# Inverting the softmax denominators of an attention kernel in a folded 128x16 tile

## What is computed

```python
xn = _layernorm(x, axis=-1)                       # x: (2, 2048, 512)
q, k, v = split(xn @ W_qkv); per head of 32
attn = q @ k.T / sqrt(32) + alibi_bias + causal_mask
y = softmax(attn) @ v                             # heads side by side, then @ W_o
x = x + y @ W_o + gate * (expert_out[argmax] + b)
```

## Time and profile before

| | us |
|---|---|
| median of three runs | 1879.65 |
| lowest, highest | 1877.83, 1888.87 |
| the profiled execution's own time | 1884.69 |
| its span, first to last instruction | 1883.1 |
| PE busy | 1731.0 (92%) |
| DVE busy | 1092.8 (58%) |
| ACT busy | 799.8 (42%) |
| POOL busy | 678.4 (36%) |
| mean granted clock of PE | 0.955 |

### The profile page before, as it was taken

How to read it: one execution, slowest core, us unless ns; L and a number is a source line. 1 busy time by engine, 2 the same in 40 slices (tenths; PEclk the granted TensorE clock), 3 DMA queues, 4 the chain that set the end, 5 groups by cost and what they waited for, 6 DMA issues and landing times. The chain is left out here.

```text
span 1883.1 us, 31814 instructions
## 1 busy us (share of the span) xinstructions
PE 1731.0 (92%) x10482; PEld 1057.3 (56%) x10483; DVE 1092.8 (58%) x1969; ACT 799.8 (42%) x1575; POOL 678.4 (36%) x668
## 2 busy tenths in 40 slices
PE   5999999568699999999999899999999999699798
PEld 4777778334254555554554555555555543588676
DVE  5333333556576766766766667766766730544365
ACT  3222222024344555555565456556555556421110
POOL 4401000036433454354355246246245346011350
PEclk8999999669899999999999899999999999899899
DMA  6766764875901801900900900720730500355594
GB/s 224 247 224 228 261 213 159 147 202 198 182 6 35 155 8 26 164 8 15 176 8 9 182 8 7 144 46 7 142 49 7 186 12 7 117 181 164 181 395 188
DMA packets 103621, 231.34 MB, mean 123 GB/s; under 512 B 10828, under 2 KB 28236, under 8 KB 97836
## 3 DMA queue, kind: packets, MB, share of 16 engines
q1 hardware_dynamic: 87736, 178.83, 36.8%
q0 software_dynamic: 15744, 50.67, 7.5%
HBM read 131.09 MB, written 97.85 MB: 122 GB/s over the span
## 5 line engine op out<-in xcount | busy, mean ns | idle before, releaser
L957 DVE TENSOR_REDUCE part_max<-max_ps 128x1 f32<-128x512 f32 (+3 forms) x1280 | 700.7, 602 | 375.5 <-PE max_ps L1068 272.6
L1038 ACT ACTIVATE probs_sb<-score_ps 128x512 f32<-128x512 f32 (+3 forms) x1280 | 620.5, 542 | 541.4 <-PE score_ps L1106 244.3
L941 POOL TENSOR_TENSOR pair_sum<-probs_sb 128x512 f32<-128x512 f32 x384 | 480.0, 1282 | 587.3 <-ACT probs_sb L1038 463.2
L1068 PE MATMUL max_ps<-k_aug,q_aug 104*128 104x512 f32 (+3 forms) x1280 | 535.5, 429 | 56.8 <-DMA q_aug<-q_rows_d 36.9
L1103 PE MATMUL score_ps<-q_aug,k_aug 106*128 106x512 f32 (+3 forms) x1280 | 523.2, 415 | 28.9 <-ACT probs_sb L1038 12.6
L1103 PEld LDWEIGHTS score_ps<-q_aug,k_aug 106*128 106x128 f32 x1280 | 251.6, 197 | 177.0 <-issue 114.9
L1068 PEld LDWEIGHTS max_ps<-k_aug,q_aug 104*128 104x128 f32 x1280 | 259.1, 203 | 131.9 <-DVE part_max L957 70.6
L1147 PE MATMUL acc_ps<-probs_sb,v_sb 128*32 128x512 f32 (+3 forms) x2560 | 293.5, 537 | 0.0
L989 DVE RECIPROCAL acc_sb<-acc_sb 128x128 f32<-128x128 f32 x128 | 119.8, 941 | 76.6 <-ACT acc_sb L1022 76.6
L1147 PEld LDWEIGHTS acc_ps<-probs_sb,v_sb 128*32 128x32 f32 x2560 | 73.5, 111 | 113.8 <-issue 98.5
L614 DVE SCALAR_TENSOR_TENSOR st_lo<-group_ps,st_hi 128x512 fp32r<-128x512 f32 x64 | 44.3, 692 | 139.6 <-ACT st_hi L661 135.0
(11 more groups left out here) (171 smaller groups left out, 1689.5 us busy)
## 6 DMA issues: line engine op xcount, KB each, us to landing
k_aug<-k_hi_d SPq DMA_DIRECT2D x14, 1024.0 KB
q_aug<-q_hi_d SPq DMA_DIRECT2D x14, 1024.0 KB
slot_x_d<-zero_f POOLq DMA_DIRECT2D x20, 512.0 KB, 5.9
rows<-slot_x_d SPq DMA_DIRECT2D x40, 256.0 KB, 2.6
slot_y_d<-y_rows POOLq DMA_DIRECT2D x39, 256.0 KB, 2.5
xn_d<-xn SPq DMA_DIRECT2D x8, 1024.0 KB, 10.3
q_hi_d<-st_hi SPq DMA_DIRECT2D x32, 256.0 KB, 7.2
q_lo_d<-st_lo SPq DMA_DIRECT2D x32, 256.0 KB, 7.1
```

The source lines that it names most:

```text
L941: nc.gpsimd.tensor_tensor(pair_sum[:, p % 2, hh], probs[:, s0, hh], probs[:, s1, hh], ALU.add).then_inc(pair_added, 1)
L957: nc.vector.tensor_reduce(part_max[:, hh * QT + i, kc:kc + 1], max_ps[:, bank, 0:w], AX.X, ALU.max).then_inc(max_taken, 1)
L1038: nc.scalar.activation(probs[:, r % P_SLOTS, hh, off:CH], score_ps[:, (r * HG + hh) % S_BANKS, off:CH], ACT.Exp).then_inc(exp_done, 1)
L1068: last = nc.tensor.matmul(max_ps[:, bank, 0:w], q_aug[0:ROW_MAX, half, hh, i * P:(i + 1) * P], k_aug[0:ROW_MAX, half, hh, kc * CH:kc * CH ...
```

## The change

The four quarter reciprocals go. ACT, after its exponentials of round 3 past a chunk's last, issues a DMA that takes the four different rows of the denominators (every 32nd partition, 512 numbers) and lays them out as 128 partitions of 16 numbers (`fold_out`, into `den_fold`). DVE inverts that tile in one instruction in round 4 past the last. In round 5 ACT issues a DMA that writes it to DRAM (`unfold`, into `inv_d`), and in round 6 one that reads each of the four rows 32 times, back over `den_sb` (`spread_rows`). POOL's product stands where it stood and waits for that last DMA. All four steps wait on semaphores of the step before. On all other engines the order stays.

```diff
@@ -147,12 +147,17 @@
 
 
 LEAVE_AT = {(LAST_ROUND[c] + 2) % NR: ((LAST_ROUND[c] + 2) // NR, c) for c in range(QC)}
-QUARTERS = 4
-INVERT_AT = {(LAST_ROUND[c] + 3 + k) % NR: ((LAST_ROUND[c] + 3 + k) // NR, c, k)
-             for c in range(QC) for k in range(QUARTERS)}
-
-Y_BEFORE_PAIR = {min([p for p in range(NPAIR) if PAIR_LAST[p] > (LAST_ROUND[c] + 3 + QUARTERS) % NR] or [NPAIR]):
-                 ((LAST_ROUND[c] + 3 + QUARTERS) // NR, c) for c in range(QC)}
+
+
+def rounds_past(n):
+
+    return {(LAST_ROUND[c] + n) % NR: ((LAST_ROUND[c] + n) // NR, c) for c in range(QC)}
+
+
+FOLD_AT, INVERT_AT, UNFOLD_AT, SPREAD_AT = rounds_past(3), rounds_past(4), rounds_past(5), rounds_past(6)
+
+Y_BEFORE_PAIR = {min([p for p in range(NPAIR) if PAIR_LAST[p] > (LAST_ROUND[c] + 7) % NR] or [NPAIR]):
+                 ((LAST_ROUND[c] + 7) // NR, c) for c in range(QC)}
 
 
 class Memory:
@@ -188,6 +193,7 @@
     m.y_d = nc.dram_tensor("y_d", [G, P, S], F32).ap()
     m.slot_x_d = nc.dram_tensor("slot_x_d", [SLOTS, D], F32).ap()
     m.slot_y_d = nc.dram_tensor("slot_y_d", [SLOT_TILES * P, D], F32).ap()
+    m.inv_d = nc.dram_tensor("inv_d", [2, HG, CH], F32).ap()
     m.k_rows_d = nc.dram_tensor("k_rows_d", [AUG_ROWS, H, S], F32).ap()
     m.q_rows_d = nc.dram_tensor("q_rows_d", [AUG_ROWS, HG, S], F32).ap()
 
@@ -755,6 +761,7 @@
         max_lo = sb("max_lo", [HG * TPC, 2, P], F32R)
         acc_sb = sb("acc_sb", [P, 2, 2, CH], F32)
         y_sb, den_sb = acc_sb[:, :, 0], acc_sb[:, :, 1]
+        den_fold = sb("den_fold", [P, 2, HG * CH // P], F32)
         score_ps = pb("score_ps", [P, S_BANKS, CH], F32)
         max_ps = pb("max_ps", [P, M_BANKS, CH], F32)
         acc_ps = pb("acc_ps", [P, 2, CH], F32)
@@ -773,6 +780,7 @@
             sem("scored"), sem("probs_ready"), sem("pv_done"), sem("pair_added"), sem("pair_used"))
         experts_loaded = sem("experts_loaded")
         accs_left, inverted, y_done = sem("accs_left"), sem("inverted"), sem("y_done")
+        folded, unfolded, spread_out = ([sem(f"{n}{i}") for i in range(2)] for n in ("den_folded", "inv_unfolded", "inv_spread"))
         xn_loaded, slots_stored = [sem("xn_loaded0"), sem("xn_loaded1")], sem("slots_stored")
         XN_TILES = 4
         AUG = 16 * 8
@@ -916,7 +924,7 @@
 
                 def normalise(g, cc):
                     n = g * QC + cc
-                    pool.wait_ge(inverted, (n + 1) * QUARTERS)
+                    pool.wait_ge(spread_out[cc % 2], 16 * (g * (QC // 2) + cc // 2 + 1))
                     nc.gpsimd.tensor_tensor(y_sb[:, cc % 2], y_sb[:, cc % 2], den_sb[:, cc % 2], ALU.mult).then_inc(y_done, 1)
 
                 def step(g, half, first, last):
@@ -982,11 +990,10 @@
                         elif kind == SPLIT:
                             low_rows(g + dg, n, banks[dg, TURN, n][0])
 
-                def invert(g, cc, k):
-
-                    dve.wait_ge(accs_left, g * QC + cc + 1)
-                    quarter = den_sb[:, cc % 2, bass.ts(k, CH // QUARTERS)]
-                    nc.vector.reciprocal(quarter, quarter).then_inc(inverted, 1)
+                def invert(g, cc):
+
+                    dve.wait_ge(folded[cc % 2], 16 * (g * (QC // 2) + cc // 2 + 1))
+                    nc.vector.reciprocal(den_fold[:, cc % 2], den_fold[:, cc % 2]).then_inc(inverted, 1)
 
                 def step(g, half, first, last):
                     events, banks = plan_of(g, last)
@@ -994,14 +1001,13 @@
                     for r in range(NR):
                         maxima(events[r], banks, g, units)
                         if r in INVERT_AT:
-                            back, cc, k = INVERT_AT[r]
+                            back, cc = INVERT_AT[r]
                             if not (first and back):
-                                invert(g - back, cc, k)
+                                invert(g - back, cc)
 
                 maxima(PLAN_BEFORE[0], BANKS_BEFORE, 0, (0, None))
                 groups(dve, step)
-                for k in range(QUARTERS):
-                    invert(G - 1, QC - 1, k)
+                invert(G - 1, QC - 1)
 
             @block.scalar
             def _(act):
@@ -1020,6 +1026,22 @@
 
                     wait_past(act, y_stored[cc % 2], 16 * (g * (QC // 2) + cc // 2))
                     nc.scalar.activation(acc_sb[:, cc % 2], acc_ps[:], ACT.Copy).then_inc(accs_left, 1)
+
+                def fold_out(g, cc):
+
+                    act.wait_ge(accs_left, g * QC + cc + 1)
+                    act.dma_start(den_fold[:, cc % 2], acc_sb[0:P:DH, cc % 2, 1]).then_inc(folded[cc % 2], 16)
+
+                def unfold(g, cc):
+                    act.wait_ge(inverted, g * QC + cc + 1)
+                    act.dma_start(m.inv_d[cc % 2].rearrange("h (s n) -> (h s) n", n=HG * CH // P),
+                                  den_fold[:, cc % 2]).then_inc(unfolded[cc % 2], 16)
+
+                def spread_rows(g, cc):
+
+                    act.wait_ge(unfolded[cc % 2], 16 * (g * (QC // 2) + cc // 2 + 1))
+                    act.dma_start(den_sb[:, cc % 2], m.inv_d[cc % 2].unsqueeze(1).to_broadcast([HG, DH, CH])).then_inc(
+                        spread_out[cc % 2], 16)
 
                 def step(g, half, first, last):
                     events, banks = plan_of(g, last)
@@ -1042,10 +1064,25 @@
                             back, done = LEAVE_AT[r]
                             if not (first and back):
                                 leave(g - back, done)
+                        if r in FOLD_AT:
+                            back, done = FOLD_AT[r]
+                            if not (first and back):
+                                fold_out(g - back, done)
+                        if r in UNFOLD_AT:
+                            back, done = UNFOLD_AT[r]
+                            if not (first and back):
+                                unfold(g - back, done)
+                        if r in SPREAD_AT:
+                            back, done = SPREAD_AT[r]
+                            if not (first and back):
+                                spread_rows(g - back, done)
 
                 maxima(PLAN_BEFORE[0], BANKS_BEFORE, 0)
                 groups(act, step)
                 leave(G - 1, QC - 1)
+                fold_out(G - 1, QC - 1)
+                unfold(G - 1, QC - 1)
+                spread_rows(G - 1, QC - 1)
 
             @block.tensor
             def _(pe):
```

## The result

The changed kernel takes 2055.65 us (median of 4 runs, 2051.14 to 2060.88). The kernel before, beside it on the same chip, takes 1881.57 us (4 runs, 1877.83 to 1888.87). The ratio is 1.092 with a 95% interval of 1.088 to 1.097: slower by 174 us. The profiled execution took 2060.88 us with a span of 2059.2, against 1883.1 before, at a mean granted clock of 0.911 (0.955 before).

The account below looks back on a forecast made before the run. PE was taken as the bound. Without the load -7 us, plus 136 for groups 1 to 6 and 6 for group 0, gave +135 on the 1883.1 us span: 2018, forecast as 2015 us, range 1864 to 2130.

Parts of the forecast that it names:

- DVE's relief: Attention stage: without the quarter reciprocals PE waits less for row maxima, 24 us gained (0 to 45).
- ACT's issues: 96 added DMA issues on ACT: 0.3 us per fold and 0.1 per unfold, 13 us in all (0 to 32).
- ACT as the bound: Rival: 96 issues of 0.57 us on ACT, all on the path, would cost 55 us; no chance given.
- The tail: End of the attention stage: three transfers and one reciprocal in place of four reciprocals, +4 us (3 to 7).
- All of it without the load: Whole kernel without any quarrel over the transfers: -24 + 13 + 4 = -7 us.
- The turns: Fold under the next group's load: 32 packets on each of four engines alternate with the load's, 20.5 us; chance 0.38.
- The rest of the fold's latency: Fold's time besides its turns, 2.4 us as for y_d; landing after 22.9 us, PE standing 16.7 us per group.
- The unfold: The write to DRAM under the load: lands after 8 turns, 7.5 us, with nothing added to the time.
- The clock: PE restarting at half clock after its stall in groups 1 to 6: 6.0 us more per group.
- not held up: Rival: the load doesn't delay the small transfers, so -7 us stands, about 1870 us; chance 0.28.
- Whole backlog: Rival: ACT's descriptors wait for all of SP's queued load, PE stands 32 us per group, 2134 us; chance 0.18.
- Fewer turns: Rival: sixteen engines or several rows per turn, fold lands after 7.5 to 12 us, 1880 to 1945 us; chance 0.16.

Follow-up runs that it names:

- h_store: b_halves with the store of a group's last y chunk issued by ACT after round 8, not by SP behind the load: 1856.43 us, ratio 0.988.
- a_small: The changed kernel with the loads for groups 2 to 7 cut to 64 of 2048 columns of q_aug and k_aug: 1862.05 us, ratio 0.995.
- x_recip_only: The kernel before with one 128x16 reciprocal per chunk in place of four of 128x128, no DMA added: 1858.24 us, ratio 0.988.
- a_k16: The changed kernel with the fold issued as four DMAs, one row each, so that 16 engines carry it: 2076.38 us, ratio 1.109.
- b_small: The kernel before with the loads for groups 2 to 7 cut to 64 of 2048 columns of q_aug and k_aug: 1870.56 us, ratio 0.999.
- a_2k: The changed kernel with the load in four slices of 512 columns, so that its packets are 2 KB: 2047.34 us, ratio 1.092.
- a_c3q: The changed kernel with chunk 3 inverted in quarters on DVE as before, chunks 0 to 2 folded: 1986.70 us, ratio 1.056.
- b_halves: The kernel before with two 128x256 reciprocals per chunk, placed in DVE's idle time, in place of four quarters: 1869.15 us, ratio 0.993.

## Why the prediction was right, and where it was off

The forecast was slower, with 2015 us; it is 2055.65. Its mechanism holds, in the order in which it was put. On the span the sum said 2018 and 2059.2 came, 41 us more. By term:

- **DVE's relief, -24.** About right in size: groups 1 to 6 of h_store are 22.7 us shorter, 3.8 each, pairs 1 to 3 most of all, and those of a_small 19.9. That x_recip_only as a whole gains 23 is in part luck, since its groups 1 to 6 give nearly all of it back at the store behind the load and keep 2.5 us; the sum hadn't seen that store.
- **ACT's issues, +13: too large.** An issue holds ACT for 0.32 us (unfold) or 0.54 to 0.56 (fold, spread), but a_small with its 12 issues per group has a period of 139.8 against 139.6 in h_store with one. The 0.3 us for each fold were hidden. That also rules out the rival "ACT as the bound". That ACT's room isn't unlimited a_k16 shows: 1.9 us more at one place cost 4.3 in pair 7, part of it by the clock.
- **The tail, +4.** From the copy at the stage's end to the product it went from 4.5 us to 9.7 (ACT 1782.02, POOL 1791.68 in the timeline): +5.1.
- **All of it without the load, -7, and +6 in group 0.** a_small's span of 1858.8 against 1865.4 in b_small is -6.6 where these make -1. By groups it is +6.0 up to the start of group 1, -19.9 in groups 1 to 6, and +7.3 behind the start of group 7. Only the middle figure is clear of noise: in group 0 and behind the start of group 7 the kernel before and b_small run the same program, and their profiled executions differ there by 10.2 and 6.8 us.
- **The turns, 20.5 us.** Right in this kernel: 128 packets in 20.2 us, as four engines would take them. This is the step that decided. Group 7 bears it out with small packets too: 3.3 us there, against 3.4 in the sum. a_2k doesn't (1.6 us in group 2), so it isn't a rule for every load. The Trainium skill (DMA: Bandwidth & Descriptors, "Why a DMA increments its semaphore by 16 and not by 1") gives 4 engines for this shape, and 16 for one row cut in 32 pieces by 32 partitions; the 4 per 0.63 us here and the 16.3 us of a_k16 agree. Its "Queues, rings and completion order" lets an engine change queues between packets of typically 9 to 17 descriptors; here the trace has one row of 64 bytes for one of 8 KB, and the measurement decides. So by that section alone the prediction's one row per turn didn't follow.
- **The rest of the fold's latency, 2.4 us: the step that was too small.** It was taken from an unloaded store. Under the load 6.9 us pass before the first packet and 3.9 after the last, 10.8 in all. PE therefore stood 24.8 us and not 16.7. Over groups 1 to 6 this pause is 22.0 to 24.8 us, 142.5 in all, against 100 in the sum: 42 too few.
- **The unfold, "I add nothing": wrong, and the smaller part.** It lands after 10.8 us, not 7.5, again with 7 us before a packet moves, and PE waits 2.6 us for it; over the six groups 16.7 us.
- **The clock, 6.0 us.** Pairs 2 and 3 take 45.8 us in group 2, against 11.9 in a_small; less the 24.8 and the 2.6 that leaves 6.5. Over the six groups the same account leaves 26 us, 4.4 a group, so there the term was 10 us too large.
- **Chunk 0's fold past the load:** right in this kernel (4.4 us), and a_c3q and a_2k show that it was the stall itself that carried it past.
- **Groups 0 and 7.** +8.2 in the changed kernel for the +6 of group 0, which by the 10.2 us above isn't clear of noise; chunk 1's unfold does take 13.0 us there. Nothing was charged to group 7, whose folds take 8.1 and 6.7 us beside the experts' weights: its pairs 2 and 4 have 7.89 and 10.79 us in place of 6.28 and 7.86.

So per group the sum had 22.7, and in group 2 it was 33.9 (45.8 - 11.9). Over groups 1 to 6, 1036.0 us against 850.6 in a_small, it is 30.9 on average, since group 4 lost less: 185 us against 136. These +49 (fold +42, unfold +17, clock -10), less the 6 by which the rest came out better, are the 41 on the span but for some 2.5 us. The range that went with the likeliest case, 1970 to 2065, held the time. Worked out again from its own ends (a turn at 0.5 to 0.8 us, the clock between 0 and 8) it would be about 1952 to 2058, which holds it by 2 us: neither the start under load nor the unfold was in it.

Of the rivals, "not held up" is out: a_small shows what it would have been (ratio 0.995). "Whole backlog" is out as put, since a_k16 has its fold at 798.9 while SP's queue keeps the engines busy for some 21 us more; but the times came near to it, because in these runs the links of the chain add up to about the length of the load whichever of them waits. "Fewer turns" would have been the case with 16 engines, and a_k16 shows that its price of 2 to 12 us per group was wrong too (33 us there, 1050.1 against 850.6 in groups 1 to 6): it left out the start-up and the unfold.

What stays open is where the 7 us before a small DMA's first packet come from. They are 6.8 to 7.3 in groups 1 to 6 with 8 KB packets and 4.7 to 8.0 in a_2k with 2 KB (6.2 in group 2), so they don't shrink by four with the size of a packet. Away from any load it is 1.2 us for a fold. No run tells apart whether the descriptors are made late or wait in the engine behind those fetched before. Open too is why a_2k's folds mostly need fewer turns than one for one.

## What to carry to other kernels

Before work is moved from an engine to a chain of small dependent DMAs, look at what else uses the 16 engines at that moment, and count each link by itself: start-up under load, what stands before it in its own queue, turns (here at most its packets per engine times the time of one of the load's packets, and the largest packets count), and completion. Here shortening one link only let a later one wait; put the chain outside the load or don't have it. And look for the same relief without a transfer: here two reciprocals placed in DVE's idle time, and one store moved out of the load's queue, gave all that the folding gave without its load.

## What the runs showed of the hardware

- Two queues with work for the same engines alternated packet by packet where the load's are of 8 KB: one of 64 bytes for one of those, 4 per 0.63 us. With the load in 2 KB packets (a_2k) the 128 small ones took 1.2 to 5.9 us, and only the slowest case was about one for one. Beside 20 rows of 32 KB, in the median 4.5 us each, the 128 packets of an unfold took 11.2 us (a_k16).
- A small DMA issued on a second queue under the load moves next to nothing at first: 6.8 to 7.3 us for the folds of groups 1 to 6, 6.8 to 7.1 in a_k16, 4.7 to 8.0 in a_2k. Without load a fold's first packet comes after 1.2 us, and half of all unfolds have landed within 1.5.
- A small DMA waits for what its own queue holds too: a_2k's fold behind a 256 KB spread had its first packet 15.7 us after the issue.
- A 256 KB store on ACT's queue under the load landed after 17.3 us in the median (h_store), soon enough, where the same store behind the load in SP's queue took up to 29.4 us (b_halves).
- A reciprocal of 128x16 takes 244 ns and one of 128x256 1739 ns, against 941 for 128x128: two halves cost 0.29 us less per chunk than four quarters.
